# A memset after every gather in place of one per group, in a graph kernel paced by GpSimd

## The reference

```
h = relu(layernorm(x))
msg[e] = h[src[e]] @ rel_weight[edge_type[e]]          # 16 relations, 64 x 64
x = x + segment_sum(msg, dst)
h = relu(layernorm(x))
msg[e] = relu([h[src[e]], h[dst[e]], edge_attr[e]] @ W1 + b1) @ W2 + b2
x = x + segment_sum(msg, dst)
```

## Time and profile before

| engine | busy us | share of the span | instructions |
|---|---|---|---|
| POOL | 3372.5 | 69% | 3742 |
| PE (matmul) | 2742.2 | 56% | 10310 |
| PE (weight load) | 1539.6 | 32% | 10310 |
| DVE | 1465.5 | 30% | 2002 |
| ACT | 577.6 | 12% | 1139 |

### The profile page before, as it was taken

The page is one execution under the profiler, slowest core; times in us unless marked ns, Lnnn a source line. Parts: engine busy times, 40 slices in busy tenths (PEclk is TensorE's granted clock), DMA queues, the critical chain, the costliest instruction groups (busy, mean ns, idle before and its releaser), DMA issues.

```text
span 4863.8 us, 37713 instructions
## 1 busy us (share of the span) xinstructions
PE 2742.2 (56%) x10310; PEld 1539.6 (32%) x10310; DVE 1465.5 (30%) x2002; ACT 577.6 (12%) x1139; POOL 3372.5 (69%) x3742
## 2 busy tenths in 40 slices
PE   2655555556555555555565646555555555556555
PEld 1433333334333333333332222222222222222222
DVE  6322222222222222222232323332323332323333
ACT  3111111111111111111110001000000010000000
POOL 7576666667667666666757777777777767777776
PEclk9777777777777777777766666666666666666666
DMA  4111111111111111111111112111112112112111
GB/s 102 21 25 25 25 27 25 25 27 25 25 27 25 25 25 27 25 25 27 25 29 28 31 30 32 29 31 31 30 30 32 29 30 31 30 30 32 29 31 28
DMA packets 391187, 144.15 MB, mean 30 GB/s; under 512 B 321650, under 2 KB 337323, under 8 KB 391163
## 3 DMA queue, kind: packets, MB, share of 16 engines
q0 software_dynamic: 106304, 109.07, 11.7%
q1 hardware_dynamic: 282245, 34.18, 4.9%
q10 hardware_dynamic: 2614, 0.62, 0.1%
HBM read 129.03 MB, written 12.83 MB: 29 GB/s over the span
## 4 chain that ended last, share of the span: by engine, by line
POOL 52%; issue 31%; another core or an unknown queue 6%; PE 5%; DVE 3%; DMA 1%; SPq 1%; POOLq 1%; DVEq 0%; ACT 0%; ACTq 0%
POOL rows L710 48%; PE ps L1379 2%; POOL spacer L743 2%; POOL spacer L763 2%; PE ps L1386 1%; DMA rows<-h_table,idx 1%; PE ps L1462 1%; PE ps L1461 1%; DVE z_slot L1230 0%; DVE q_blk L1243 0%; DVE slots L1219 0%; POOLq L359 0%; PE ps L1466 0%; DVEq L1234 0%
## 5 line engine op out<-in xcount | busy, mean ns | idle before, releaser
L710 POOL DMA_INDIRECT rows<-p_table,idx x1661 | 1576.2, 949 | 702.9 <-issue 629.5
L710 POOL DMA_INDIRECT rows<-h_table,idx x1533 | 1448.2, 945 | 711.7 <-issue 514.9
L1379 PE MATMUL ps<-onehot,rows 128*64 128x256 f32 x3328 | 676.7, 568 | 619.3 <-DMA rows<-h_table,idx 518.8
L1461 PE MATMUL ps<-w_attr,attr_t 64*128 64x512 f32 x416 | 407.2, 1079 | 1001.6 <-DVE q_blk L1243 714.9
L1095 DVE TENSOR_TENSOR onehot<-key,ps 128x2048 f32<-128x2048 f32 x209 | 475.5, 2278 | 656.5 <-remote 428.5
L1379 PEld LDWEIGHTS ps<-onehot,rows 128*64 128x64 f32 x3328 | 354.2, 200 | 861.5 <-issue 792.9
L1219 DVE TENSOR_TENSOR slots<-ps,rows 128x512 f32<-128x512 f32 x208 | 143.9, 692 | 1427.1 <-DMA rows<-p_table,idx 881.8
L1386 PE MATMUL ps<-w_types,slots 128*128 128x128 f32 x3328 | 466.2, 295 | 95.6 <-issue 91.9
L1386 PEld LDWEIGHTS ps<-w_types,slots 128*128 128x128 f32 x3328 | 427.3, 207 | 171.2 <-issue 163.5
L1461 PEld LDWEIGHTS ps<-w_attr,attr_t 64*128 64x128 f32 x416 | 98.0, 292 | 1039.2 <-issue 1039.1
L1462 PE MATMUL ps<-q_blk,onehot 128*128 128x512 f32 x416 | 423.5, 1121 | 0.0
(11 more groups left out here) (142 smaller groups left out, 1874.2 us busy)
## 6 DMA issues: line engine op xcount, KB each, us to landing
rows<-p_table,idx POOLq DMA_INDIRECT x1661
rows<-h_table,idx POOLq DMA_INDIRECT x1533
attr<-in_edge_attr_dram SPq DMA_DIRECT2D x52, 128.0 KB
q_win<-q_table SPq DMA_DIRECT2D x208, 32.0 KB
p_table<-pq_out SPq DMA_DIRECT2D x25, 120.0 KB
q_table<-pq_out SPq DMA_DIRECT2D x25, 120.0 KB
out_dram<-xs SPq DMA_DIRECT2D x25, 120.0 KB
xs<-in_x_dram SPq DMA_DIRECT2D x6, 480.0 KB, 6.3
```

The source lines that it names most:

```text
L710: pool.indirect_dma_start(rows[:, u, t, :], None, table, bass.IndirectOffsetOnAxis(ap=at, axis=0)).then_inc(s, 16)
L1379: last = pe.matmul(slot_ps[t % 2 * D:(t % 2 + 1) * D, b, t // 2, :], rows[:, u, t, :], onehot[:, b, t, :], start=True, stop=True)
L1461: pe.matmul(pre_ps[:, u % 2, :], attr_t[half, u // 2, :], w_attr[half].rearrange("k j d -> k (j d)"), start=True, stop=False)
```

## The change

The memset of 512 columns behind every group and the wait for it ahead of the next group go. Instead a function `space(n, width)` follows every gather: it waits until n memsets of this kind have finished (the semaphore starts at 1, so `spaced` >= n + 1), that is, until the memset behind the *previous* gather has finished, and then issues a memset of `width` columns. The width is 3 * D = 192 in layer 1 and 2 * D = 128 in layer 2. So in place of 400 memsets of 512 columns there are 1533 of 192 columns and 1661 of 128 (one per gather of the two loops). The counter n is worked out from the loop's register, the group and the tile. The semaphore's first increment moves up ahead of the first gathers, and the scratch tile shrinks to 192 columns. The gathers, their order and all waits on other engines stay.

```diff
-        spacer = sb("spacer", [P, T * D], fp32)
+        spacer = sb("spacer", [P, 3 * D], fp32)
...
+            def space(n, width):
+
+                wait_apart(pool, spaced, n + 1)
+                pool.memset(spacer[:, 0:width], 0.0).then_inc(spaced, 1)
+
+            pool.sem_inc(spaced, 1)
             pool.wait_ge(first_idx, 1)
...
-                pool.sem_inc(spaced, 1)
-
                 def turn_of_rows(it, last=False):
                     for u in range(U):
-                        wait_apart(pool, spaced, (it - 2) * U + u + 1)
 
                         if u % B == 0:
                             wait_apart(pool, batch_in[u // B], 16 * (it - 1))
                         wait_apart(pool, slots_summed, 2 * AHEAD + 2 * (it * U + u - 1))
                         for t in range(SKIP if last and u == U - 1 else 0, T):
                             gather(h_table, u, t, rows_in[u])
-                        pool.memset(spacer[:], 0.0).then_inc(spaced, 1)
+                            space(((it - 2) * U + u) * T + t - (SKIP if last and u == U - 1 else 0), 3 * D)
...
                 def turn_of_groups(it, last=False):
                     for u in range(U):
-                        wait_apart(pool, spaced, (NIT - 2 + it) * U + u + 1)
...
                         wait_apart(pool, pre_added, it * U + u + AHEAD - 1)
                         for j in range(SKIP if last and u == U - 1 else 0, T):
                             gather(p_table, u, j, rows_in[u])
-                        pool.memset(spacer[:], 0.0).then_inc(spaced, 1)
+                            space(((NIT - 2 + it) * U + u) * T + j - (2 if last and u == U - 1 else 1) * SKIP, 2 * D)
```

## The result

The changed kernel took 4949.99 us (median of 4 runs, 4949.48 to 4954.51); the kernel before, run beside it on the same chip, 4866.9 us. The ratio is 1.0175, with a 95% interval of 1.0157 to 1.0193: slower by 1.75%. The prediction was 4944 us. The time is right to 6 us, and most of what the prediction said of how it comes about is wrong; this is what the rest is about.

The account below looks back on a forecast made before the run. POOL's own pace was taken as the bound. Layer 1 +92, layer 2 +8, group starts -15 and PE waits -10 gave +75 us on 4866.0, then 3.5 more: 4944 us, range 4840 to 5120.

Parts of the forecast that it names:

- The bound now: Both loops: POOL's own pace, 11.20 us a group, is the bound, in layer 2 almost alone.
- What the change removes: Group ends in both loops: 1.20 us a group, 480 us for 400 groups, plus 15 us of later starts.
- The new wait: Behind each gather: wait, increment and register addition cost nothing, covered by the gather itself.
- third rival: Every gather pays 0.90 us behind its memset, near 7050 us; chance 0.09, shared with a dearer instruction refetch.
- The memset in POOL's stream: Behind each gather: the 0.305 us gap stays, the memset adds 0.21 us (192 columns) or 0.155 us (128).
- first rival: The gap before each gather hides the memset; layer 2 at 10.0 us a group, 4576 us in all; chance 0.08.
- What is late next is the same engine: After the change POOL stays the bound; transfers, SP's queue, PE, ACT and DVE lose nothing.
- PE's pace may follow the spacing of the rows more than their number: Layer 1: given as a way the forecast could be wrong, without a size.
- Even spacing frees layer 1: Layer 1: rows arrive in step, all 70.6 us of PE waits go, 4841 us in all; chance 0.16.
- Instruction code: POOL's turn roughly doubles in instructions; one or two more stalls per turn, +40 to +80 us, inside the range.

Follow-up runs that it names:

- e1: Kernel before without its 512-column memset per group and the wait for it, in both layers, nothing in their place: 5135.3 us, ratio 1.0587.
- e7: Kernel without any spacer, with less PE work (8 of 16 relation matrices, no w_attr product): 5065.0 us, 1.0261 of the kernel before.
- e4: Changed kernel with POOL's waits on PE (layer 1) and DVE (layer 2) loosened from two groups before to four: 4943.2 us, ratio 1.0180.
- e12: Kernel without spacer, only four of each group's eight gathers issued in both loops, output not the reference's: 2851.8 us.
- e9: Changed kernel with memsets of 224 columns in both layers: 4912.7 us, ratio 1.0115 to the kernel before.
- e10: Kernel before without spacer in layer 2, where PE multiplies a constant tile twice more per group as filler: ratio 1.0221.
- e11: Kernel without spacer, only the last of each group's eight gathers issued in both loops, output not the reference's: 2784.2 us.

## Why the prediction was right and wrong

**The bound now.** Right: POOL's own pace set layer 2 (36 us over it) and most of layer 1 (89 us over it).

**What the change removes.** Right: 1.20 us a group, and the later starts at u = 0 and 4 (the median start of a group is now that of any gather, 1.39 and 1.34 us).

**The new wait.** Rightly costed at nothing: the memset starts at once when the gather ends. The third rival (0.9 us per gather) is refuted by the same rows.

**The memset in POOL's stream.** Wrong, and first in the sum. "In a row of gathers part of the way is already walked ahead, and what is left should be POOL's own work. I therefore let it stand behind the memset." It doesn't: the gap behind a memset is 0.165 us, not 0.305. So memsets recorded at 0.275, 0.22 and 0.30 us (192, 128 and 224 columns) add 0.14, 0.09 and 0.17 us to the pitch; 0.13 us of each lies in the gap. I had 0.21 and 0.155. Of the first rival this half was true. The Trainium skill's rule (Perfetto Trace Analysis, "GPSIMD Engine Instruction") is to time GpSimd by start-to-start spacing and not by spans. The trace agrees in so far as a memset recorded at 0.22 us moves the starts of gathers only 0.09 us further apart. With this term right and the rest of my sum as it was, layer 1 would have been 15 us shorter and layer 2 100 us: 4866 - 115 - 15 - 10 + 3.5, some 4730 us, a forecast on the wrong side.

**"What is late next is the same engine."** Wrong for layer 2, and it made up for the first error. I took POOL to stay the bound and POOL's waits for PE in layer 1 to shrink by 10 us. Instead those waits grew, from 70.6 to some 110 us beyond the usual gap (59 waits, 120 us in all, less 0.17 us each), and the loss over POOL's own pace rose by 39 us in layer 1 and 158 in layer 2. So +92 in layer 1 was -15 + 39 = +23, and +8 in layer 2 was -100 + 158 = +58. With the starts and waits I had some +75 in layer 1 and nothing in layer 2. The sum came to +82 where I had +75, by luck. The sentence on layer 1 that PE's pace may follow the spacing of the rows more than their number, given as a way to be wrong, came nearest.

**The first rival's price**, 4576 us, rested on layer 2 at 10.0 us a group. e1 ran just that stream and took 5135. The preparation had shown 11.5 us a group without a spacer in layer 1, and I used it for layer 1 alone; it spoke of a chain that doesn't follow POOL. So did, in layer 2, with DVE waiting 9.32 us for something "remote": I read it only for POOL's start.

**Even spacing frees layer 1** (fourth rival): no; POOL's waits there went up. Its sum had a slip besides: 8 x (1.25 + 0.14) is 11.12 us, not 11.16, so its time would have been some 4832 us in place of 4841. **Instruction code** (fifth): no. 18 packets against 14 in the whole run, for a POOL stream of nearly twice the instructions, and the late gather of 0.8 us per turn is as it was. The stall that the Trainium skill describes for a taken branch (Runtime: NRT & Kernel Launch, "Instruction fetch mechanics") shows in no row, unless the unexplained late gather is one; 14 or 18 packets in 50 turns leave no room for a fetch in each turn.

**What stays open.** Why PE's results come up to 20 us after their recorded ends. Neither the amount of PE's work (e7), nor a deeper lead of POOL (e4), nor the DMAs' whole traffic (e12), nor long waits as such (e9) explains it; more work in the gaps may take a third of the loss away (e10). Long bursts of gathers, by their transfers or by POOL's work beside PE, remain as a rival that no run here varied apart from POOL's pace. The Trainium skill (TensorE: Matmul & The Clock Gate, "Seeing it yourself") warns that the records of the clock on trn2 are not reliable and that the clock has been seen held below its usual low level for over 50 us. No run here shows it: the records of this case know only 1.2 and 2.4 GHz. It might be a part. At half the lower level the two products before 3639.30, recorded at 4.05 us from start to end, would take 8.1 us (an estimate from these records); the increment came after 10.3. No version of mine beats the kernel before: on the curve of the table, layer 2 is shortest at 11.20 us a group of the paces tried, with 2366 us; 21 of its 36 us over own pace are the late gathers, so little is left to gain there by pace alone.

## What to carry to other kernels

A delay put in on purpose is a pace: cost it first by what the stream's pace becomes, and then by who has to keep up with it. Before calling an engine the bound, find the row that shows how long the engines behind it take when they are fed at once; here no row of the kernel before did in layer 2, and a run with half the gathers gave it (7.6 us a group). And a forecast that hits the time can have two wrong terms in it; check the pitch, the waits and each layer, not only the sum.

## What the runs showed of the hardware

- A memset behind a row gather of 128 x 256 bytes hides 0.13 us of its time in the 0.305 us gap ahead of the next one, at 128, 192 and 224 columns alike.
- A wait on POOL's own earlier memset, with an increment and a register addition, costs nothing behind a gather of 0.95 us.
- The late second gather at u = 6 (0.8 us, once per turn) is there in every kernel with a spacer, with 1 or 8 memsets a group. Without a spacer it is gone from layer 1 of e1, and there in 2 of 26 turns of its layer 2 (in e10 in 8 of 26). It comes at one fixed place of POOL's stream; its cause isn't shown.
- Results of PE can come far later than the recorded ends of their matmuls say: in layer 2 of the changed kernel the semaphore's increment is over 5 us behind in 33 of 170 cases, at most 14.8 us. In e9, e11 and e12 it is never more than 0.01 us behind.
- The kernel before took 4745 to 4934 us from batch to batch, a spread of 4%, and only leaving the spacer out weighs more; two kernels have to be compared in one batch.
